# Moving first-batch weight work of GpSimd between the two low halves of Wo and Wv

## The reference

```python
# x: (4, 1024, 512); Wq, Wk, Wv, Wo: (512, 512)
def attn(x):
    q, k, v = x @ Wq, x @ Wk, x @ Wv                    # (b, s, f)
    scores = einsum('bse,bsf->bef', q, k) / sqrt(16)     # features against features
    return swap(softmax(scores) @ swap(v)) @ Wo
def ffn(h):                                              # 512 -> 2048 -> 512
    gate_w, up_w, down_w = spline(gate_cp), spline(up_cp), spline(down_cp)
    return (silu(h @ gate_w.T) * (h @ up_w.T)) @ down_w.T
x = x + layernorm(attn(layernorm(x)))
x = x + layernorm(ffn(layernorm(x)))
```

## Time and profile before

| | us |
|---|---|
| median of 3 runs | 756.93 |
| lowest, highest | 756.38, 761.38 |
| the profiled execution | 758.16 |
| its span, first to last instruction | 756.4 |
| granted TensorE clock, mean | 0.955 |

### The profile page before, as it was taken

How to read it: one execution, slowest core, us unless ns; L and a number is a source line. 1 busy time by engine, 2 the same in 40 slices (tenths; PEclk the granted TensorE clock), 3 DMA queues, 4 the chain that set the end, 5 groups by cost and what they waited for, 6 DMA issues and landing times. The chain is left out here.

```text
span 756.4 us, 16316 instructions
## 1 busy us (share of the span) xinstructions
PE 676.6 (89%) x5872; PEld 476.1 (63%) x5872; DVE 512.7 (68%) x993; ACT 365.5 (48%) x635; POOL 430.7 (57%) x615
## 2 busy tenths in 40 slices
PE   5996799999999999989947699898989899898996
PEld 3685686878687887867723255565655566564565
DVE  7666773588646973575656668887878878774653
ACT  3532232333232432333335677776777677574641
POOL 5269858547681958910425556564656546554642
PEclk9899899999999999999967899999999999998999
DMA  6814547324561447411786827567394946548123
GB/s 228 309 56 156 182 169 249 119 77 144 190 217 59 159 159 250 138 53 25 209 219 188 186 66 178 131 178 172 123 191 134 206 120 183 123 120 183 63 71 98
DMA packets 65549, 114.98 MB, mean 152 GB/s; under 512 B 12624, under 2 KB 29136, under 8 KB 65488
## 3 DMA queue, kind: packets, MB, share of 16 engines
q1 hardware_dynamic: 65488, 114.16, 52.4%
HBM read 81.76 MB, written 32.37 MB: 151 GB/s over the span
## 5 line engine op out<-in xcount | busy, mean ns | idle before, releaser
L1328 POOL TENSOR_TENSOR act<-inter,act 128x512 f16<-128x512 f32 x128 | 149.6, 1169 | 135.1 <-ACT act L1369 135.0
L1373 ACT ACTIVATE gated<-gbank,c_gate 128x512 f32<-128x512 f32 x128 | 88.0, 687 | 104.0 <-PE gbank L1542 104.0
L1442 DVE SCALAR_TENSOR_TENSOR inter<-ubank,c_up,gated 128x512 f32<-128x512 f32 x128 | 95.6, 747 | 49.8 <-ACT gated L1373 47.8
L1583 PE MATMUL ybank<-down,act 128*128 128x160 f16 x512 | 112.2, 238 | 0.0
L1584 PE MATMUL ybank<-down,act 128*128 128x160 f16 x512 | 111.5, 237 | 0.0
L1585 PE MATMUL ybank<-down,act 128*128 128x160 f16 x512 | 111.4, 236 | 0.0
L1369 ACT CAST act<-inter 128x512 f16<-128x512 f32 x128 | 78.2, 611 | 1.7 <-DVE inter L1442 1.7
L1583 PEld LDWEIGHTS ybank<-down,act 128*128 128x128 f16 x512 | 50.7, 99 | 39.2 <-issue 35.4
L1542 PE MATMUL gbank<-z,s_all 128*32 128x512 f16 x512 | 53.3, 407 | 24.3 <-DMA z<-token_features 15.9
L1542 PE MATMUL ubank<-z,s_all 128*32 128x512 f16 x512 | 52.7, 402 | 8.3 <-DVE inter L1442 7.5
L1584 PEld LDWEIGHTS ybank<-down,act 128*128 128x128 f16 x512 | 51.0, 100 | 3.8
(11 more groups left out here) (195 smaller groups left out, 1943.5 us busy)
## 6 DMA issues: line engine op xcount, KB each, us to landing
x_ln<-x SPq DMA_DIRECT2D x64, 256.0 KB, 3.5
z<-token_features SPq DMA_DIRECT2D x64, 256.0 KB, 5.9
job<-job_in SPq DMA_DIRECT2D x24, 640.0 KB, 4.3
shared<-x SPq DMA_DIRECT2D x32, 256.0 KB, 2.7
x<-shared SPq DMA_DIRECT2D x32, 256.0 KB, 2.0
token_features<-z_hi SPq DMA_DIRECT2D x32, 256.0 KB, 4.2
x_res<-x SPq DMA_DIRECT2D x32, 256.0 KB, 2.7
out<-x_res SPq DMA_DIRECT2D x32, 256.0 KB, 2.1
```

Source lines behind the costliest of these rows:

```text
L1328: pool.tensor_tensor(hidden[par][:, i, TOK:2 * TOK], inter[:, i % INTERS, :], hidden[par][:, i, 0:TOK], ALU.subtract).then_inc(inter_ready, 1)
L1373: act.activation(gated[:, slot % 2, :], gbank[:], ACT.Silu, scale=c_gate[:]).then_inc(silu_done, 1)
L1442: dve.scalar_tensor_tensor(out=inter[:, i % INTERS, :], in0=ubank[:], scalar=c_up[:], in1=gated[:, i % 2, :], op0=ALU.mult, op1=ALU.mult). ...
L1583: pe.matmul(out, hidden[par][:, r, high], box[:, 0], start=False, stop=False)
```

## The change

GpSimd sums job 0 right after its reduce, ahead of the low half of Wo, and does the product of unit chunk 0 and the sum of job 1 between the low halves of Wo and Wv. In `first_body`, chunk 0 starts with its sums; jobs 2 and 3 take the place of jobs 0 and 1; the two sides of chunk 1's product are parted by a scale; the scales of tiles 1 to 4 stand ahead of the pieces of chunk 1, and only the multiply of job 4, its add and the multiply of job 5 stand between the scales of tiles 5 to 7, the add of job 5 behind them. On SP the loads of jobs 2 and 3 go from behind the stores of chunk 0 to ahead of the residual loads. The number of instructions doesn't change.

```diff
--- before.py
+++ after.py
@@ -255,17 +255,17 @@
                     sp.wait_ge(xn_normed, B * NT)
                     for m in range(XR):
                         feats.load(sp, x1_t, m, m)
+                first = isinstance(b, int) and b == 0
                 if not more:
                     load_job(b, 2)
                     load_job(b, 3)
                 store_units(2 * b, True)
-                if more:
+                if more and not first:
                     load_job(b, 2)
                     load_job(b, 3)
-                else:
+                elif not more:
                     load_job(b, 4)
                     load_job(b, 5)
-                first = isinstance(b, int) and b == 0
                 if first:
                     load_x(b + 1, XR)
                     load_x(b + 1, XR + 1)
@@ -326,6 +326,8 @@
             load_w(3, wvT)
             for t in range(XR):
                 load_x(1, t)
+            load_job(0, 2)
+            load_job(0, 3)
             sp.wait_ge(wov_done, 2)
             for t in range(XR):
                 load_res(0, t)
@@ -377,10 +379,10 @@
                 unit_sum(c)
                 unit_split(c)
 
-            def unit_product(c):
+            def unit_product(c, sides=(0, 1)):
 
                 pool.wait_ge(units_loaded, (c + 1) * 32)
-                for w in range(2):
+                for w in sides:
                     pool.tensor_tensor(units[:, w], units[:, w], ucoef[:], ALU.mult).then_inc(unit_step, 1)
 
             def unit_sum(c):
@@ -427,21 +429,27 @@
             def first_body(b):
 
 
+
                 ln_scale(b + 1, 0)
-                unit_weights(2 * b)
-                sum_job(b, 0)
-                sum_job(b, 1)
-                unit_product(2 * b + 1)
+                unit_sum(2 * b)
+                unit_split(2 * b)
+                sum_job(b, 2)
+                sum_job(b, 3)
                 ln_scale(b + 1, 1)
+                unit_product(2 * b + 1, (0,))
+                ln_scale(b + 1, 2)
+                unit_product(2 * b + 1, (1,))
+                ln_scale(b + 1, 3)
                 unit_sum(2 * b + 1)
-                ln_scale(b + 1, 2)
+                ln_scale(b + 1, 4)
                 unit_split(2 * b + 1)
-                for t in range(3, NT):
+                for t in range(5, NT):
                     ln_scale(b + 1, t)
-                    if t > 3:
-                        add_job(b, t - 2)
-                    if t - 1 < JOBS:
-                        multiply_job(b, t - 1)
+                    if t == 6:
+                        add_job(b, 4)
+                    else:
+                        multiply_job(b, 4 + t // 7)
+                add_job(b, 5)
                 for t in range(NT):
                     y_scale(b, t)
 
@@ -477,10 +485,14 @@
             pool.wait_ge(max_part, 1)
             pool.partition_all_reduce(call[:], cmax[:], P, bass.bass_isa.ReduceOp.max).then_inc(max_all, 1)
 
+            sum_job(0, 0)
             for n in range(2):
                 pool.wait_ge(wov_hi_done, n + 1)
                 pool.tensor_tensor(w_lo[WO + n], w_stage[n], f32(w_hi[WO + n]), ALU.subtract
                                    ).then_inc(wov_done, 1)
+                if n == 0:
+                    unit_product(0)
+                    sum_job(0, 1)
             pool.wait_ge(scale_step, 10)
             first_body(0)
             with pool.Fori(1, B - 1) as b:
```

## The result

The changed kernel took 767.86 us (median of 4 runs, 765.27 to 770.95) against 759.15 of the kernel before beside it: ratio 1.0139, 95% interval 1.0092 to 1.0185. With more runs, in another session, it was 767.13 against 759.29, ratio 1.010, 1.0034 to 1.0166. It is slower by some 1.2%; 759.9 was forecast, and 763.5 was the top of the range.

What follows compares the result with a forecast made beforehand. Batch 0, 15.1 us longer than batch 1, was taken as all the change can touch, through the second split's end. 2.1 + 0.4 + 0.5 = 3.0 us gave 761.2 profiled, 759.9 on the median; range 757.5 to 762, tenths outside 755.2 and 763.5.

Steps and rivals of the forecast that it cites:

- What bounds the kernel: Batch 0, 15.1 us longer than batch 1: the second split's end sets the y products 16.3 us later through queued loads.
- GpSimd not to be had before 33.48: After GpSimd's reduce in batch 0: no next instruction before 33.48, whichever it is, so the Wv low half ends 3.8 us later.
- 28.35 - 3.27 + 1.64 = 26.7: GpSimd from Wv low half to second split: first product out, two scales of 0.82 in; split 2.1 us later.
- the 0.5 for the clock in the softmax: TensorE, waiting for late exponentials, has a short low-clock stretch slowing the Wo product: 0.5 us, at most 1.8.
- Behind the split: SP's chain unchanged: job 4 comes 11.3 us after the split, GpSimd stands about 10, y products 2.1 us late.
- The 0.4 for the clock ahead of y: TensorE's longer stop before the y products changes its low-clock stretch: 0.4 us, between 1.7 back and 1.7 more.
- The clock case: Rival: TensorE at its lower level some 7 us in the softmax and again ahead of y; 5.6 us, 762.5, chance 0.14.
- The base: Starting time the loss was added to: 758.16 us for the profiled execution, 756.93 as median of the runs.

Runs made afterwards that it cites:

- The freed tail: Changed kernel with x tiles 6 and 7 loaded before chunk 1's stores, jobs 4 and 5 between y scales, batch 1's job loads later: 752.33 us, ratio 0.9926.

## Why the prediction was wrong

- **What bounds the kernel: right.** The loss that can be placed lies in batch 0 and comes through the chain that was read backwards there: the split, SP's queue, job 4's load, the scale of tile 6, the y products. The freed tail shows it from the other side.
- **GpSimd not to be had before 33.48: right.** The sum of job 0 started at 33.41, and at 34.52 in another order. From the reduce's end to the next instruction were 6.7 to 8.0 us in the twelve profiles. The Trainium skill's 5.95 us ("GPSIMD Engine Reference", section 2.1), which the page gives for the first call to freshly loaded code and without the event wait, is short as a price of this place; whether it is the same cost is not shown. The Wv low half was 3.4 late (3.8 forecast).
- **The step that failed: "28.35 - 3.27 + 1.64 = 26.7", GpSimd's work to the end of the second split, with the 0.5 for the clock in the softmax.** The row took 30.6. The product is out, as said (3.27). But five scales take 5.3 us where three took 2.4: those of tiles 1 to 3 cost 1.03 to 1.35 each and not some 0.8 as in the row taken, 1.25 us more than reckoned in all, since they run beside VectorE's norm, as the scale of tile 4 did before. And two scales waited 2.60 us for statistics (1.88 in the second profile), against 0.5 for the clock with a top of 1.8: the sum took a low stretch to be mostly hidden behind GpSimd's row, but the new order put these two scales where the row has to wait for the slowed Wo product. So the split was 5.7 late and not 2.6.
- **Behind the split: right.** 11.6 us to job 4's multiply (11.3), GpSimd standing 10.86 (about 10), y resuming 6.0 late with the split 5.7 late. The 0.4 for the clock ahead of y lies between two executions: from the y products' resuming to batch 1 the changed kernel took 0.3 less than before in one and 1.2 more in the other.
- **The rivals.** The clock case, 2.1 + 1.8 + 1.7 = 5.6, came nearest in size: its place in the softmax was right (0.50 granted for 10 us) and its price there, 1.8, near the waits of 2.60 and 1.88; the dearer scales were in no rival. It had 0.14.
- **The base.** The sum was tied to a median of 756.93 from three runs and to one profile. More runs of the same kernel gave 757.67 and 759.29, and two more profiles 762.6 and 761.0. So some 2 us of the miss are the base. Of the 8.0 us between 759.9 and 767.9, 2.9 are batch 0 (5.9 for 3.0) and 2.2 the base that was measured beside it (759.15); the other 2.9 lie within the spread of four runs.

## What to carry to other kernels

Work put into an idle gap is free only up to the gap's length: 3.07 us in the hole of 5.66 shortened batch 0, and the change's 9.43 put the Wv low half 3.4 us back, with everything that waits for it. Before small pieces are moved on an in-order engine, follow what the next-but-one load waits for. Here the move was paid for at a load queued behind the end of the very work that was delayed, and freeing that load's neighbours (two x loads ahead of the stores, two jobs between the y scales, the next batch's job loads later) was worth 13.7 us of batch 0. And take a base from more than one profile where executions differ by 6 us.

## What the runs showed of the hardware

- GpSimd gave no instruction of its ordinary kind for 6.7 to 8.0 us behind the partition reduce, whichever instruction came next and whether what it waited for was there or not.
- A scale on GpSimd, two instructions of 128x1, took 0.8 us in some places and 1.3 in others of the same program, with no wait shown (0.19 and 0.55 against 0.37 to 0.43 and 0.88). Every one of the 38 dear ones in batch 0 of the twelve profiles overlapped VectorE's norm or `z_lo`, and none of the 58 cheap ones did.
- TensorE's low level came and went in one part of an unchanged program by execution: its first low stretch at the start of the feed-forward phase, read in steps of 1 us, was 20.5 us long in two executions of the kernel before and 17.1 in the third. The span from batch 3 to the end differed by 6.2 us between these executions, and not with this stretch: the one with 17.1 took 460.6 us, those with 20.5 took 455.1 and 461.3. What makes the difference was not shown.
